# Two mixtures of experts, each as one stage over all four images, with the weights multiplied into the inner units

## The reference, cut to what matters

```python
def _L2_ffn_ref(x, Wr, br, W1, b1, g1, be1, m1, v1, W2, b2, g2, be2, m2, v2, Wo, bo):   # 8 experts
    feat = jnp.mean(x, axis=0)          # weights are the same for all images
    w = jax.nn.softmax(feat @ Wr + br, axis=-1)
    h = jnp.einsum('bfd,edh->bfeh', x, W1) + b1
    h = jax.nn.relu(_bn(h, g1, be1, m1, v1))
    h = jnp.einsum('bfeh,ehk->bfek', h, W2) + b2
    h = jax.nn.relu(_bn(h, g2, be2, m2, v2))
    y = jnp.einsum('bfeh,ehd->bfed', h, Wo) + bo
    return jnp.einsum('bfed,fe->bfd', y, w)

# _L3_ffn_ref, after the graph attention has given topk_i and w; 4 experts, 256 inner units
for ei in range(NUM_EXPERTS):
    g = jnp.where(topk_i == ei, w, 0.0).sum(-1)
    hh = jax.nn.gelu(x @ W1[ei] + b1[ei], approximate=False)
    out = out + g[..., None] * (hh @ W2[ei] + b2[ei])

t = t + _L2_ffn_ref(_ln_t(t), ...)
t = t + _L3_ffn_ref(_ln_t(t), ...)
x = _from_tokens(t, x)              # back to channels x pixels
```

## Time and profile before

| what | value |
|---|---|
| median of three runs | 2987.98 us (2985.31 to 2989.21) |
| the profiled execution, its time | 2991.07 us |
| the profiled execution, its span in the trace | 2989.4 us |
| instructions in the trace | 27474 |
| batch-normed mixture | 1229 to 1488.2 us of the span |
| gelu mixture | 2826.9 us to the end of the span |

### The profile page before, as it was taken

How to read it: one execution, slowest core, us unless ns; L and a number is a source line. 1 busy time by engine, 2 the same in 40 slices (tenths; PEclk the granted TensorE clock), 3 DMA queues, 4 the chain that set the end, 5 groups by cost and what they waited for, 6 DMA issues and landing times. The chain is left out here.

```text
span 2989.4 us, 27474 instructions
## 1 busy us (share of the span) xinstructions
PE 1912.7 (64%) x8712; PEld 882.0 (30%) x8712; DVE 1711.1 (57%) x4040; ACT 968.2 (32%) x1547; POOL 575.2 (19%) x611
## 2 busy tenths in 40 slices
PE   1664873883793766787638888787886410280188
PEld 1222321321331434444312222232222210280166
DVE  3576786776776644467725756656662120188522
ACT  1232232141142122243315666565664210000123
POOL 2200500600500300000012222322223157400000
PEclk8777886896796867798758999998897655555589
DMA  3202100201200000000020111010100021000000
GB/s 87 74 17 52 33 17 27 56 8 35 56 2 21 1 0 0 10 17 17 14 64 23 36 33 35 17 52 15 33 5 6 7 62 10 6 37 0 2 15 15
DMA packets 54204, 76.12 MB, mean 25 GB/s; under 512 B 17536, under 2 KB 28794, under 8 KB 53818
## 3 DMA queue, kind: packets, MB, share of 16 engines
q1 hardware_dynamic: 43556, 65.05, 7.5%
q10 hardware_dynamic: 6426, 7.99, 1.2%
q0 software_dynamic: 4096, 1.58, 0.8%
HBM read 46.00 MB, written 24.71 MB: 24 GB/s over the span
## 5 line engine op out<-in xcount | busy, mean ns | idle before, releaser
L2145 DVE TENSOR_REDUCE f_half_max<-f_ring 128x1 f32<-128x512 f32 x512 | 335.1, 685 | 310.8 <-PE f_ring L1820 308.6
L2028 ACT ACTIVATE f_probs<-f_ST 128x512 f32<-128x512 f32 x512 | 292.9, 597 | 217.3 <-PE f_ST L1844 213.3
L1820 PE MATMUL f_ring<-f_stacks 96*128 96x512 bf16 x512 | 213.4, 418 | 54.6 <-DVE f_half_max L2145 27.8
L772 DVE TENSOR_REDUCE att_half_max<-att_ring 128x1 f32<-128x512 f32 x256 | 161.2, 684 | 102.5 <-PE att_ring L659 93.7
L1844 PE MATMUL f_ST<-f_stacks 99*128 99x512 bf16 x512 | 204.3, 404 | 11.8 <-ACT f_probs L2028 11.8
L2938 PE MATMUL ts_ps<-ts_tally 128*64 128x64 bf16 x1024 | 96.9, 354 | 166.8 <-issue 145.3
L755 ACT ACTIVATE att_probs<-att_ST 128x1024 f32<-128x1024 f32 x128 | 129.3, 1023 | 156.7 <-PE att_ST L684 156.5
L2973 DVE TENSOR_SCALAR ts_tally<-ts_digits 128x256 bf16<-128x256 bf16 x512 | 78.0, 231 | 164.6 <-PE ts_ps L2938 107.4
L1861 PE MATMUL f_O<-f_probs,f_v_ext 128*32 128x512 f32 x1024 | 155.6, 684 | 0.1
L1474 ACT ACTIVATE bm_h<-mx_ps,bn 128x512 f32<-128x512 f32 x128 | 99.5, 777 | 138.9 <-PE mx_ps L1468 117.9
L2938 PEld LDWEIGHTS ts_ps<-ts_tally 128*64 128x64 bf16 x1024 | 91.1, 258 | 172.5 <-issue 150.9
(11 more groups left out here) (550 smaller groups left out, 3552.8 us busy)
## 6 DMA issues: line engine op xcount, KB each, us to landing
f_stacks<-f_parts SPq DMA_DIRECT2D x192, 64.0 KB, 2.2
parts_dram<-l_parts SPq DMA_DIRECT2D x8, 768.0 KB, 4.1
stacks<-parts_dram SPq DMA_DIRECT2D x24, 256.0 KB, 9.4
stacks<-parts_dram ACTq DMA_DIRECT2D x24, 256.0 KB, 10.6
f_parts<-f_parts SPq DMA_DIRECT2D x8, 768.0 KB, 3.6
es_raw<-L_ffn_edge_index SPq DMA_DIRECT2D x8, 512.0 KB, 4.5
xn_cm<-x SPq DMA_DIRECT2D x1, 2048.0 KB
left_codes<-es_last SPq DMA_DIRECT2D x4, 512.0 KB, 2.7
```

The source lines that it names most:

```text
L772: nc.vector.tensor_reduce(half_max[:, h % 2, t, n:n + 1], ring[:, i % RING], AX.X, ALU.max, negate=True).then_inc(reduced, 1)
L1820: nc.tensor.matmul(ring[:, i % RING], f.stacks[0:STACK, 0, at, t * P:(t + 1) * P], f.stacks[0:STACK, 1, at, n * BANK:(n + 1) * BANK], star ...
L2028: nc.scalar.activation(f.probs[:, s % PROBS, n * BANK:(n + 1) * BANK], ST[:, i % HALVES], ACT.Exp).then_inc(probs_ready, 1)
L2145: nc.vector.tensor_reduce(f.half_max[:, h % 2, t, n:n + 1], ring[:, i % RING], AX.X, ALU.max, negate=True).then_inc(reduced, 1)
```

## The change

Each mixture becomes one stage over all images; a "run" is one expert of one image (32 runs of the batch-normed mixture, 16 of the gelu mixture). The weight is no longer applied to the output but to the inner units, before the output product, so that the products of all experts of an image add up in PSUM. For that the weights must be known on all 128 partitions: they are written to DRAM and read back with a broadcast, 4 KB a row, into `mix` [128, 8, 1024] and `gates_wide` [128, 4 images, 4 experts, 1024].

In `batch_normed_mixtures` GpSimd does that multiplication in place, on halves of 128x512, and the output products come two runs after the hidden ones (`LAG` = 2, three buffers `h2`). The hidden ring is four banks; two pairs of banks take the outputs of even and odd images. The bias product opens each image's accumulation in the same bank. VectorE does the steps of all four list parts in one stream and adds an image's two banks to `t_tm` once, two runs into the next image. SyncE's queue is one as well: the weights to DRAM, the first part's loads, eight broadcasts, then loads and stores of the parts in turn.

In `gelu_mixtures` VectorE multiplies both halves of the inner units (128x2x512) by the gate. The output product has `x2` as the stationary operand and 512 token columns moving, so its result has channels on partitions; the residual `t_tm` enters the same bank through four products with the identity, and `turn_image` is gone. VectorE copies the finished bank to `xn_cm` and SyncE stores it in halves. In `choose_experts` the transposes and the copy are gone and 16 broadcasts are added to SyncE's queue, inside that stage.

```diff
@@ -1364,119 +1364,124 @@
...
-def mixture(nc, k, xc, t_tm, weight, weight_t, experts, bias, hidden, out_parts, beside=None):
...
+def batch_normed_mixtures(nc, k):
     with ExitStack() as c:
...
+        LAG = 2
+        r = Routing()
+        r.by_owner, r.found = sb("by_owner", [P, BY_OWNER]), sb("found", [P, LIST])
+        parts = [part(nc, k, c, r) for part in (FirstLists, ClassLists, OwnerLists, OwnedSlots)]
+        mix, h1, h2 = sb("bm_mix", [P, E1, N]), sb("bm_h1", [P, N]), sb("bm_h2", [P, LAG + 1, N])
+        ps = c.enter_context(psum(nc, "bm_ps", [P, 8, BANK], F32))
...
+        mix_in, of_part = sems[:E1], [sems[E1 + 4 * i:E1 + 4 * i + 4] for i in range(len(parts))]
+        HIDDEN, runs = 4, B * E1
+        def out_bank(b, u):
+            return ps[:, HIDDEN + 2 * (b % 2) + u]
+        def half(x, u):
+            return chunk(h2[:, x % (LAG + 1)], u)
         @block.tensor
         def _(pe):
...
+            def hidden(x, i):
+                b, e = divmod(x, E1)
+                g = 4 * x + i
+                if g >= HIDDEN:
+                    pe.wait_ge(hidden_off, g - HIDDEN + 1)
+                if i < 2:
+                    w1, inner = k.m1[:, e], chunk(k.xn_cm[:, b], i)
+                else:
+                    pe.wait_ge(hidden_off, 4 * x + i - 1)
+                    w1, inner = k.m2[:, e], chunk(h1, i - 2)
+                nc.tensor.matmul(ps[:, g % HIDDEN], w1, inner, start=True, stop=True).then_inc(hidden_ready, 1)
+            def out(x, u):
+                b, e = divmod(x, E1)
+                bank = out_bank(b, u)
+                if e == 0:
+                    if b >= 2:
+                        pe.wait_ge(added, 2 * (b - 2) + u + 1)
+                    for t in range(4):
+                        nc.tensor.matmul(bank[:, t * P:(t + 1) * P], chunk(k.mix_t, 4 * u + t, P), k.mo_b[:],
+                                         start=(t == 0), stop=False)
+                pe.wait_ge(weighed, 2 * x + u + 1)
+                for t in range(4):
+                    last = nc.tensor.matmul(bank[:, t * P:(t + 1) * P], chunk(half(x, u), t, P), k.mo[:, e], start=False,
+                                            stop=(e == E1 - 1 and t == 3))
+                if e == E1 - 1:
+                    last.then_inc(out_ready, 1)
+            for x in range(runs + LAG):
+                for u in range(2):
+                    if x < runs:
+                        hidden(x, 2 * u)
+                        hidden(x, 2 * u + 1)
+                    if x >= LAG:
+                        out(x - LAG, u)
...
         def _(act):
...
+            for x in range(runs):
+                e = x % E1
+                for i in range(4):
+                    j, n = divmod(i, 2)
+                    act.wait_ge(hidden_ready, 4 * x + i + 1)
+                    nc.scalar.activation(chunk(h1, n) if j == 0 else half(x, n), ps[:, (4 * x + i) % HIDDEN], ACT.Relu,
+                                         bias=k.bn[:, j, 1, e:e + 1], scale=k.bn[:, j, 0, e:e + 1]).then_inc(hidden_off, 1)
+        @block.sync
+        def _(sp):
+            sp.dma_start(k.mix_dram, k.mix_t[:]).then_inc(mix_out, 16)
+            parts[0].load(sp, of_part[0][0])
+            sp.wait_ge(mix_out, 16)
+            for e in range(E1):
+                sp.dma_start(mix[:, e], k.mix_dram[e].partition_broadcast(P)).then_inc(mix_in[e], 16)
+            for i, (part, (loaded, listed, left, stored)) in enumerate(zip(parts, of_part)):
+                if i >= 1:
+                    part.load(sp, loaded)
+                part.store(sp, listed, left, stored)
+        @block.gpsimd
+        def _(pool):
+            for x in range(runs):
+                b, e = divmod(x, E1)
+                for u in range(2):
+                    if b == 0:
+                        pool.wait_ge(mix_in[e], 16)
+                    pool.wait_ge(hidden_off, 4 * x + 2 + u + 1)
+                    nc.gpsimd.tensor_tensor(half(x, u), half(x, u), chunk(mix[:, e], u), ALU.mult).then_inc(weighed, 1)
         @block.vector
         def _(dve):
...
+            link = linker(dve, chained)
+            def lists():
+                for part, (loaded, listed, left, stored) in zip(parts, of_part):
+                    yield from part.steps(dve, link, loaded, listed, left)
+            def add(b, u):
+                rows = k.t_tm[:, b, 4 * u:4 * u + 4].rearrange("p t n -> p (t n)")
+                dve.wait_ge(out_ready, 2 * b + u + 1)
+                nc.vector.tensor_tensor(rows, out_bank(b, u), rows, ALU.add).then_inc(added, 1)
+            steps = lists()
+            for x in range(runs):
+                b, e = divmod(x, E1)
                 for u in range(2):
...
-class Hidden:
...
-def batch_normed_mixture(nc, k, b, beside):
...
+                    next(steps, None)
+                    if b >= 1 and e == LAG:
+                        add(b - 1, u)
+            for _ in steps:
+                pass
+            for u in range(2):
+                add(B - 1, u)
...
@@ -2328,42 +2333,95 @@
...
-def gelu_mixture(nc, k, b, out):
+def gelu_mixtures(nc, k, out):
     with ExitStack() as c:
...
-            turn_image(nc, k, ps, t_tm, xc)
...
-                sp.dma_start(out[b].rearrange("c h w -> c (h w)"), xc).then_inc(k.stored, 16)
...
+        ps = c.enter_context(psum(nc, "gm_ps", [P, 8, BANK], F32))
...
+        HIDDEN, runs = 4, B * E2
+        def out_bank(b, n):
+            return ps[:, HIDDEN + 2 * (b % 2) + n]
+        def columns(x, n):
+            return hid[:, x % 2, :, n * BANK:(n + 1) * BANK]
+        @block.tensor
+        def _(pe):
+            def hidden(x, n):
+                b, e = divmod(x, E2)
+                for half in range(2):
+                    g = 4 * x + 2 * n + half
+                    if g >= HIDDEN:
+                        pe.wait_ge(hidden_off, g - HIDDEN + 1)
+                    nc.tensor.matmul(ps[:, g % HIDDEN], k.x1[:, e, half * P:(half + 1) * P], chunk(k.xn_cm[:, b], n),
+                                     start=True, stop=True).then_inc(hidden_ready, 1)
+            def product(x, n):
+                b, e = divmod(x, E2)
+                bank = out_bank(b, n)
+                if e == 0:
+                    if b >= 2:
+                        pe.wait_ge(out_off, 2 * (b - 2) + n + 1)
+                    for t in range(4):
+                        nc.tensor.matmul(bank[:, t * P:(t + 1) * P], k.t_tm[:, b, 4 * n + t, :], k.ident[:],
+                                         start=(t == 0), stop=False)
+                    nc.tensor.matmul(bank, k.x2_b[:], chunk(k.gates_t[:, b], n), start=False, stop=False)
+                pe.wait_ge(weighed, 2 * x + n + 1)
+                for half in range(2):
+                    last = nc.tensor.matmul(bank, k.x2[:, e, half], columns(x, n)[:, half], start=False,
+                                            stop=(e == E2 - 1 and half == 1))
+                if e == E2 - 1:
+                    last.then_inc(out_ready, 1)
+            pe.wait_ge(k.late, 48)
+            pe.wait_ge(k.gates_t_in, 16)
+            for x in range(runs + 1):
+                for n in range(2):
+                    if x < runs:
+                        hidden(x, n)
+                    if x >= 1:
+                        product(x - 1, n)
+        @block.scalar
+        def _(act):
+            for x in range(runs):
+                e = x % E2
+                for n in range(2):
+                    for half in range(2):
+                        g = 4 * x + 2 * n + half
+                        act.wait_ge(hidden_ready, g + 1)
+                        at = C_B1 + 2 * e + half
+                        nc.scalar.activation(columns(x, n)[:, half], ps[:, g % HIDDEN], ACT.Gelu,
+                                             bias=k.cols[:, at:at + 1]).then_inc(hidden_off, 1)
+        @block.vector
+        def _(dve):
+            def carry_off(b, n):
+                dve.wait_ge(out_ready, 2 * b + n + 1)
+                nc.vector.tensor_copy(chunk(k.xn_cm[:, b], n), out_bank(b, n)).then_inc(out_off, 1)
+            for x in range(runs):
+                b, e = divmod(x, E2)
+                for n in range(2):
+                    dve.wait_ge(k.gates_in[x], 16)
+                    dve.wait_ge(hidden_off, 4 * x + 2 * (n + 1))
+                    gate = chunk(k.gates_wide[:, b, e], n).unsqueeze(1).broadcast_to([P, 2, BANK])
+                    nc.vector.tensor_tensor(columns(x, n), columns(x, n), gate, ALU.mult).then_inc(weighed, 1)
+                    if b >= 1 and e == 1:
+                        carry_off(b - 1, n)
+            for n in range(2):
+                carry_off(B - 1, n)
+        @block.sync
+        def _(sp):
+            for b in range(B):
+                image = out[b].rearrange("c h w -> c (h w)")
+                for n in range(2):
+                    sp.wait_ge(out_off, 2 * b + n + 1)
+                    sp.dma_start(chunk(image, n), chunk(k.xn_cm[:, b], n)).then_inc(k.stored, 16)
...
```

(89 more changed lines are left out.)

71 lines of the change are left out of this document (7 added, 64 removed).

## The result

The kernel after takes 2893.62 us (median of 4 runs, 2889.75 to 2895.61) against 2988.60 (4 runs, 2985.31 to 2990.25): a ratio of 0.9682, 95% interval 0.9665 to 0.9699. That is 3.2% faster, 95.0 us, where 109 were forecast. The profiled executions took 2991.07 and 2889.75 us, 101.3 apart; the first was the highest of its kernel's runs and the second the lowest of its own, so 6 us of the 14 that are missing between the medians are put down to scatter of whole executions. The other 8 are in the two stages and in the chain that leads into the second.

The account below looks back on a forecast made before the run. TensorE was nearly the bound in the batch-normed stage's first image, VectorE in the third, with restarts between; TensorE was busy in running gelu. 2991.07 - 78.3 - 31.2 = 2881.6, forecast as 2879 us after allowing for run scatter; range 2868 to 2904.

Parts of the forecast that it names:

- Batch-normed stage: First product to last addition of the batch-normed mixtures: 178.7 us against 257.0, a gain of 78.3.
- the bias: Bias products on TensorE in the batch-normed stage: 4 x 16 x 0.112 = 7.2 us.
- GpSimd at no cost: 64 products of 128x512 in the batch-normed stage, 1272 ns each, 2.6 us a run against 5.23: cost 0.
- The rival that the two engines hinder each other: Batch-normed stage: GpSimd and VectorE work adds, about 200 us instead of 178.7, total 2900; chance 10%.
- Lists: VectorE's list steps in the batch-normed stage: hidden beside TensorE, with some 8 to 10 us of cover.
- The chain into the gelu stage: choose_experts: 16 added SyncE issues at 0.45 us cancel the dropped transposes and copy; same start, about 2827.6.
- the rival in which SyncE's queue holds the stage back: Before the gelu stage: queue takes only some broadcasts at once; 85 us more, 2965, or 2900 if half; chance 8%.
- Gelu stage: Gelu mixture: 6.84 us a run, 109.5 for 16 runs, TensorE 126.5, end at 2958.2; gain 31.2 us.
- The identity and bias products: TensorE in the gelu stage: identity 1.8 and bias 1.7 us for each image, 14.0 in all.
- The end behind TensorE: After the gelu stage's last product: signal 0.3, a copy of 0.69, and 3.1 us behind that copy.
- The rest goes into the four restarts: Batch-normed stage before: time beyond the runs, of 257.0 us, goes to bias stage, half-clock start, barrier, SyncE's stores and loads.
- the bound in the middle of the third image: Batch-normed stage before, third image: VectorE's list steps and additions, 5.7 us a run, were taken to set the pace.

Follow-up runs that it names:

- pool_twice: Kernel after, but GpSimd multiplies each half by the weights twice in the batch-normed stage: 2738.82 us, ratio 0.9658 to the kernel before; batch-normed part 185.3 us.
- late_gates: Kernel after with the 16 gate broadcasts moved from choose_experts into the gelu stage's SyncE program: 2721.28 us, ratio 0.9599 to the kernel before; end part 139.6 us.
- stage_per_image: Kernel after with the batch-normed mixture as four stages, one per image, one list part each: 2744.60 us, ratio 0.9691 to the kernel before; batch-normed part 189.6 us.
- vector_weighs: Kernel after with VectorE instead of GpSimd multiplying the inner units behind each list step: 2747.73 us, ratio 0.9701 to the kernel before; batch-normed part 198.4 us.
- lag_one: Kernel after with LAG = 1 instead of 2: 2735.19 us, ratio 0.9650 to the kernel before; batch-normed part 186.9 us.

## Why the prediction was right, and by how much it was off

The forecast's mechanism held, and the time lies within its range. Its terms, by the profiled executions:

- **Batch-normed stage**: 178.7 forecast, 180.7 measured. The period of a run is 5.22 for 5.23. TensorE needs 1410.76 - 1230.82 = 179.9 for 177.7. The mis-sized term is the bias: a half with it takes 1244.06 - 1240.17 = 3.89 from one hidden product to the next, where a plain one takes 1250.56 - 1247.95 = 2.61. That is 1.28 us for eight records counted at 0.112 (0.90) each, all eight halves are like it, and 8 x 0.38 = 3.0 us. The first run took 5.58 for 6.30, which gives 0.7 of it back.
- **GpSimd at no cost**: right. 64 products at a mean of 1305 ns against 1272 forecast; the second product in pool_twice cost 2.3 us, the 1.41 of waiting at the end among them. The rival that the two engines hinder each other is refuted as a price, not as a mechanism: they do (last section), in places that have room.
- **Lists**: VectorE's last step ended at 1400.5 for 1397, and the additions waited 9.48 us for TensorE: the cover of 8 to 10 was there.
- **The chain into the gelu stage**: the step that failed. I had 17 issues at 0.45 us and a start that stays where it was, some 10 us behind the first issue of the gates; it lies 14.5 behind it. The median issue took 0.50 us, but the longest 2.51: the rival in which SyncE's queue holds the stage back came true in small, 4.0 us instead of 85. Its cause as I put it, a queue that accepts only some of the transfers at once, fits the spread of the issues but is not shown; that the 11.7 us lay on the path is shown by late_gates.
- **Gelu stage**: from its start to the end of the span 132.9 for 130.6. Run period and half-clock start are as forecast (the first twelve records take 7.8 us; at 0.43 they would be 5.2). The identity and bias products cost 17.1 over the four images, not 14.0: a half with them takes 2768.46 - 2762.89 = 5.57 for 3.43, eight times. The end behind TensorE was 1.0 shorter than I had it.

2.0 + 4.0 + 2.3 = 8.3 us, and the profiled gain fell 8.2 short of the forecast (101.3 for 109.5). The other 6 us between the medians are the scatter told of above; where in these executions it lies, and why the fourth layer scatters, stays open.

Two readings of the kernel before need a word; no term hung on either. "The rest goes into the four restarts" names the right place, but the restarts had their price from the additions and the bias stage: stage_per_image still restarts between images and loses 6.6 us. And VectorE was not the bound in the middle of the third image: the first hidden products there start 5.62 us apart (1373.63, 1379.25), as in the first image, with a wait of 0.17 for ScalarE and none for VectorE. VectorE's 5.7 a run made it fall behind, and TensorE met that only at the image's last outputs. So the steady period gained 0.40 us a run, put down to the order of the products, and most of the gain lay between the images.

## What to carry to other kernels

A weighted sum over experts goes into PSUM if the weights are multiplied into the operand; that takes the additions from the busy engine and leaves TensorE to set the pace. Here it was worth, together with the bias inside the accumulation, the new order and the single stage, four fifths of the stage's gain. The multiplication belongs on an engine whose queue holds nothing that can wait on something else, even a slower one: a 1.27 us product with nothing ahead of it beat a faster one behind list steps. DMA issues that the next stage's first product doesn't need are put behind that stage's barrier, since issuing alone took 12 us here. Where a stage ends in a barrier, look first at what the other engines still have to do when the dense engine is through: the turn between two images took 5.7 us where VectorE had nothing left, and 16 to 22 in the kernel before, bias stage included.

## What the runs showed of the hardware

**GpSimd and VectorE on one port.** VectorE's rows in the kernel after, at 1252, beside two products of GpSimd (duration ns min/median/max, start, form):

```profile
L2586 DVE TENSOR_SCALAR fl_whole<-fl_columns x1: 1642/1642/1642, 1252.7 to 1252.7; 128x1024 int32<-128x1024 f32 x1
L2588 DVE TENSOR_SCALAR fl_whole<-fl_whole x1: 1647/1647/1647, 1254.4 to 1254.4; 128x1024 int32<-128x1024 int32 x1
L2590 DVE TENSOR_SCALAR fl_whole<-fl_whole x1: 695/695/695, 1256.1 to 1256.1; 128x1024 int32<-128x1024 int32 x1
```

The same operation on the same shape takes 1.65 us beside a product and 0.70 a moment later, when GpSimd is idle; in vector_weighs, where GpSimd is idle, it takes 0.68. In pool_twice, with GpSimd busy all the time, a step of 128x96 that otherwise takes 0.32 takes 1.20 to 1.31, about as long as a product of GpSimd (1.27), while MAX8 does not mind:

```profile
L2728 DVE SCALAR_TENSOR_TENSOR os_banded<-os_banded,band_low x4: 1204/1206/1306, 1382.9 to 1398.0; 128x96 f32<-128x96 f32 x4
```
```profile
1299.05 0.96 DVE L2796 MAX8 cl_list<-cl_x 128x8 f32<-128x768 f32 x1
...
1301.11 0.96 DVE L2796 MAX8 cl_list<-cl_x 128x8 f32<-128x768 f32 x1
```

The Trainium skill, SBUF — State Buffer, section "SBUF: two separate sides", calls the port pair that the two engines share an exclusive lock: the one that starts first holds it for its whole instruction, and a VectorE instruction takes part only with two SBUF inputs or in a two-port mode. The trace agrees: MAX8, with one input, is as long as in the kernel before (0.96 for 0.95), and the step of 128x96, with two, is not. Whether the TENSOR_SCALAR rows, which read one tile, ran in a two-port mode no row shows.

**The length of one gap doesn't settle what the clock does.** After long unbroken work TensorE ran at full speed behind the 1.05 us between stage_per_image's stages, and at the lower level (0.50) behind vector_weighs' wait of 4.73. But in the same kernel the records behind a wait of 3.43 still ran at a granted clock of 1.00, and those behind a further 1.78 at 0.50. In lag_one a single wait of 1.82, some 5 us after the half-clock start had ended, was followed by 0.50. In the kernel before, in the second image's last outputs, two waits of 1.95 came one after the other: the products behind the first ran at full speed (1.13 for eight), those behind the second at half (2.05).

**Many large transfers issue unevenly.** Sixteen issues of 512 KB in a row took 0.34 to 2.51 us each on SyncE, and landed 4.6 to 16.2 us later (median 12.3), where the same shape alone, one record each, took 5.8 in the kernel before and 3.7 in the kernel after. Eight in a row, at the batch-normed stage's start, took 5.6 us to issue.
